# Attention on one core: scores issued three query blocks ahead instead of two

## The reference

```
q, k = rope(x @ w_aq), rope(x @ w_ak);  v = x @ w_av
s = q k^T / 128, causal mask;  p = softmax(s);  r = (p v) @ w_ao
x = layernorm(x + r)
h = silu(x W1' s1) * (x W2' s2);  h = gelu(h H1' g1);  h = gelu(h H2' g2)
x = layernorm(x + h W3' s3)
```

## Time and profile before

| what | value |
|---|---|
| three runs | 1079.12 us median (1076.83 to 1079.99) |
| the profiled execution | 1077.77 us, its span 1076.0 us |
| mean granted TensorE clock | 0.979 |
| TensorE matmul busy | 995.9 us, 93% of the span |
| VectorE busy | 852.0 us, 79% |
| ScalarE busy | 655.7 us, 61% |
| GpSimd busy | 584.5 us, 54% |
| first scores of head 0 / start of feed-forward | 29.28 us / 785.53 us |

### The profile page before, as it was taken

How to read it: one execution, slowest core, us unless ns; L and a number is a source line. 1 busy time by engine, 2 the same in 40 slices (tenths; PEclk the granted TensorE clock), 3 DMA queues, 4 the chain that set the end, 5 groups by cost and what they waited for, 6 DMA issues and landing times. The chain is left out here.

```text
span 1076.0 us, 20027 instructions
## 1 busy us (share of the span) xinstructions
PE 995.9 (93%) x5648; PEld 859.3 (80%) x5648; DVE 852.0 (79%) x1803; ACT 655.7 (61%) x1383; POOL 584.5 (54%) x536
## 2 busy tenths in 40 slices
PE   2799999999999999999999999999839999999995
PEld 1588888888888888888888888888728878788784
DVE  4888888988889898888888888888755668486744
ACT  4577676777767677777767777777625252343531
POOL 3777777777777877767787777777350101000000
PEclk8799999999999999999999999999969999999998
DMA  7542223432223223232222222221020000000000
GB/s 249 167 137 60 69 61 88 153 89 59 60 69 73 63 58 91 58 77 64 76 49 58 60 60 70 69 68 40 1 79 1 1 1 21 0 19 0 1 20 20
DMA packets 33292, 66.16 MB, mean 61 GB/s; under 512 B 5456, under 2 KB 6992, under 8 KB 32208
## 3 DMA queue, kind: packets, MB, share of 16 engines
q1 hardware_dynamic: 30400, 58.62, 20.6%
q10 hardware_dynamic: 2832, 6.82, 1.7%
HBM read 24.26 MB, written 7.34 MB: 29 GB/s over the span
## 5 line engine op out<-in xcount | busy, mean ns | idle before, releaser
L720 POOL TENSOR_SCALAR probs<-probs,inv_sum 128x128 f32<-128x128 f32 (+7 forms) x256 | 236.7, 925 | 173.5 <-DVE inv_sum L635 173.5
L537 ACT ACTIVATE pT<-psum 128x512 fp32r<-128x512 f32 (+3 forms) x384 | 176.0, 490 | 131.2 <-PE psum L404 130.1
L311 PE MATMUL psum<-pT,vals 128*128 128x512 f32 (+3 forms) x1152 | 242.2, 350 | 1.6 <-DVE rT L678 1.6
L525 ACT ACTIVATE probs<-psum,neg_max 128x128 f32<-128x128 f32 (+7 forms) x256 | 190.3, 744 | 48.8 <-DVE neg_max L629 46.9
L645 DVE TENSOR_TENSOR pT<-psum,pT 128x512 fp32r<-128x512 f32 (+3 forms) x384 | 199.8, 547 | 14.8 <-ACT pT L537 11.8
L311 PEld LDWEIGHTS psum<-pT,vals 128*128 128x128 f32 x1152 | 187.3, 189 | 24.0 <-DVE pT L645 1.7
L629 DVE TENSOR_REDUCE neg_max<-psum 128x1 f32<-128x128 f32 (+7 forms) x256 | 190.4, 744 | 3.7 <-PE psum L395 3.7
L404 PE MATMUL psum<-ident,probs 128*128 128x128 f32 x1152 | 174.6, 276 | 12.8 <-POOL probs L720 6.4
L725 POOL TENSOR_TENSOR swapped<-swapped,rope 128x512 f32<-128x512 f32 x128 | 165.4, 1292 | 37.2 <-DMA swapped<-proj 37.1
L901 PE MATMUL ps<-hid,w 128*128 128x512 f32 x768 | 181.3, 396 | 0.0
L901 PEld LDWEIGHTS ps<-hid,w 128*128 128x128 f32 x768 | 143.8, 188 | 34.4
(11 more groups left out here) (78 smaller groups left out, 1267.9 us busy)
## 6 DMA issues: line engine op xcount, KB each, us to landing
swapped<-proj SPq DMA_DIRECT2D x256, 128.0 KB, 2.3
w_stage<-qk_split SPq DMA_DIRECT2D x30, 256.0 KB, 2.6
wv_stage<-v_split SPq DMA_DIRECT2D x15, 256.0 KB, 2.6
x_split<-ffn_raw ACTq DMA_DIRECT2D x2, 1024.0 KB, 5.9
ffn_raw<-g SPq DMA_DIRECT2D x2, 1024.0 KB, 8.1
x_moving<-x_split SPq DMA_DIRECT2D x2, 1024.0 KB, 5.9
out<-y SPq DMA_DIRECT2D x4, 512.0 KB, 2.6
raw_x<-xT SPq DMA_DIRECT2D x3, 512.0 KB, 11.5
```

The costliest lines, as they stand in the source:

```text
L311: ins = nc.tensor.matmul(out_ap, left[a], right[b], start=first and i == 0, stop=last and i == 2)
L525: nc.scalar.activation(probs[:, ib % 4, :width].rearrange("p (h c) -> p h c", h=halves), score_ps[:, ib % 2, :halves, :half], ACT.Exp, bia ...
L537: nc.scalar.activation(pT[chunk][:, 0, 4 * f:4 * f + n_blocks, (ib % 4) * P:(ib % 4 + 1) * P], bank("t", head[1], nth)[:, :n_blocks * P].r ...
L720: nc.gpsimd.tensor_scalar(p, p, inv_sum[:, n:n + 1], 1.0, ALU.mult, ALU.mult).then_inc(probs_ready[0], 1)
```

## The change

LOOK = 3 takes the place of a written-out 2: TensorE issues scores of block s+3 in step s, ScalarE and VectorE follow (exp and 1/sum of block s+2, maximum of block s+3). GpSimd's product of probabilities with 1/sum stays at block s+1. Every step of the rotation moves one step forward; tile 1 and tile 2 are still projected at the steps 0 and 2, tile 0 moves to the last step of the head before, and tile 3 from step 2 to step 3. On VectorE the order inside a step is now sum of the rotation, maximum, 1/sum. The two banks are lent one step sooner, and the order in which the shared banks go round follows from the planner. One more step is put ahead of the first head.

```
+LOOK = 3
-QK_STEP = (0, 0, 2, 2)
-COS_STEP = (0, 0, 2, 2)
-SIN_STEP = (1, 2, 3, 4)
-SUM_STEP = (2, 3, 4, 6)
-HIGH_STEP = (3, 4, 6, 8)
-LOW_STEP = (3, 4, 6, 8)
+QK_STEP = (-1, 0, 2, 3)
+COS_STEP = (-1, 0, 2, 3)
+SIN_STEP = (0, 1, 3, 4)
+SUM_STEP = (1, 2, 4, 5)
+HIGH_STEP = (2, 3, 5, 6)
+LOW_STEP = (2, 3, 5, 7)
 V_STEP = (4, 5, 6, 6)
 PV0_PIECES = {6: range(0, 2), 7: range(2, 4)}
 PV1_PIECES = {1: range(0, 2), 2: range(2, 4), 3: range(4, 8)}
-LEND1 = (6, 7, 0)
-LEND3 = (1, 2)
+LEND1 = (5, 6, 7)
+LEND3 = (0, 1)
+QK_AHEAD = [1 - step // NI for step in QK_STEP]
...
-            ib, tile_off = (s + 2) % NI, off + (s + 2) // NI
+            ib, tile_off = (s + LOOK) % NI, off + (s + LOOK) // NI
...
-                     + [("qk", off + 1, j) for j in range(NQK) if QK_STEP[j] == s]
+                     + [("qk", off + QK_AHEAD[j], j) for j in range(NQK) if QK_STEP[j] % NI == s]
...
+        body((-1, 0), NI - 1, 0)
         for s in range(NI):
             body((-1, 1), s, 0)
...
 TensorE
-                if before_first(head) and s == NI - 2:
+                if before_first(head) and s == NI - LOOK:
                     pe.wait_ge(masks_ready, 1)
                     pe.wait_ge(vo_low, 1)
                 if exists(ahead):
-                    scores(ahead, (s + 2) % NI)
+                    scores(ahead, (s + LOOK) % NI)
...
 ScalarE
-                if before_first(head) and s == NI - 2:
+                if before_first(head) and s == NI - LOOK:
                     save_weights()
...
                 if exists(ahead):
-                    exponentiate(ahead, (s + 1) % NI)
+                    exponentiate(ahead, (s + LOOK - 1) % NI)
...
 VectorE
-                if exists(step_on(head, (s + 1) // NI)):
-                    inverse_sum(step_on(head, (s + 1) // NI), (s + 1) % NI)
                 for target, j in rope_tasks(head, s, SUM_STEP):
                     rope_sum(target, j)
-                if exists(step_on(head, (s + 2) // NI)):
-                    negative_max(step_on(head, (s + 2) // NI), (s + 2) % NI)
+                if exists(step_on(head, (s + LOOK) // NI)):
+                    negative_max(step_on(head, (s + LOOK) // NI), (s + LOOK) % NI)
+                if exists(step_on(head, (s + LOOK - 1) // NI)):
+                    inverse_sum(step_on(head, (s + LOOK - 1) // NI), (s + LOOK - 1) % NI)
```

More of the change, by code:

```diff
@@ L277, in before_first @@
     def before_first(head):
-        return isinstance(head[0], int) and head[0] < 0
+        return isinstance(head[0], int) and number(head) == -1
     def pair_exists(pair):
@@ L285, in bank, with qk_use @@
         return psum[:, USES[use][0] * BANK:(USES[use][0] + 1) * BANK]
+    def qk_use(head, j):
+        off = (parity(head) - QK_AHEAD[j]) % 2
+        return "qk", off + QK_AHEAD[j], j
     def wait_for_banks(pe, pair, *use):
@@ L408, in project_qk @@
             def project_qk(running, nth):
-                head = step_on(running, 1)
+                head = step_on(running, QK_AHEAD[nth])
                 if nth == 0:
@@ L454, in step @@
             def step(head, s, b):
-                ahead = step_on(head, (s + 2) // NI)
+                ahead = step_on(head, (s + LOOK) // NI)
                 if before_first(head) and s == 1:
@@ L471, in step @@
                 for target, j in rope_tasks(head, s, QK_STEP):
-                    project_qk(step_on(target, -1), j)
+                    project_qk(head, j)
                 for c in v_tasks(head, s):
@@ L546, in copy_projected @@
                 wait_for(act, rope_low, step_on(head, -1), j)
-                nc.scalar.activation(proj[:, j % 2], bank("qk", 1 if parity(head) else 2, j),
+                nc.scalar.activation(proj[:, j % 2], bank(*qk_use(head, j)),
                                      ACT.Copy).then_inc(proj_copied[0], 1)
@@ L566, in step @@
             def step(head, s, b):
-                ahead = step_on(head, (s + 1) // NI)
+                ahead = step_on(head, (s + LOOK - 1) // NI)
                 if before_first(head) and s == 1:
@@ L573, in step @@
                         high_of_x(b)
-                if before_first(head) and s == NI - 2:
+                if before_first(head) and s == NI - LOOK:
                     save_weights()
-                if before_first(head) and s == NI - 1:
+                if before_first(head) and s == NI - LOOK + 1:
                     act.wait_ge(vo_low, 1)
@@ L652, in times_cos @@
                 wait_for(dve, rope_done, step_on(head, -1), j)
-                nc.vector.tensor_tensor(by_cos[:, j], bank("qk", 1 if parity(head) else 2, j),
+                nc.vector.tensor_tensor(by_cos[:, j], bank(*qk_use(head, j)),
                                         rope[:, 0, c * BANK:(c + 1) * BANK],
```

## The result

| what | before | after |
|---|---|---|
| runs, four of each, interleaved | 1079.03 us (1076.83 to 1079.99) | 1110.32 us (1107.40 to 1114.21) |
| the profiled execution, its span | 1077.77, 1076.0 us | 1107.6, 1105.8 us |
| mean granted TensorE clock | 0.979 | 0.975 |
| first scores of head 0 | 29.28 us | 32.91 us |
| first scores of head 2 | 76.74 us | 84.96 us |

The ratio is 1.0293 with an interval of 1.0258 to 1.0328: slower by 31 us. I had forecast 1096.5 with a range of 1075 to 1114: the sign was right and the range held it, but the loss is almost twice my +17.5.

What follows compares the result with a forecast made beforehand. TensorE sets the time, and only its own waits can be won. New waits of 2.8 us a pair for 1.7 give +1.1 x 15.5 = +17, plus 0.5 for filling: 1095.3 profiled, 1096.5 on the median's scale; range 1075 to 1114.

Steps and rivals of the forecast that it cites:

- (1): Steady state: TensorE's old waits, 1.7 us a pair, go if nothing takes their place.
- (4): Even head, step 6: second fill of transposes waits for bank 1, still to be read by ScalarE; 0.5 us.
- (2): Odd head: blocks 7 and 1 share score bank 2, so block 1 waits for maximum and exp 7; 1.1 us.
- (3): Even head, step 5: second fill of transposes waits for bank 5, whose VectorE reader is late; 0.5 us.
- (5): Rotation chain through GpSimd: odd-head transposes wait 0.4 us at step 6, then 0.3; step 2 taken as nothing.
- (6): SyncE: swaps go out singly, tile 0's behind a value-projection wait and the value weights; projected early enough, so nothing.
- (7): Filling: tile 2's copy waits for the first sum, VectorE idles some 0.6 longer; +0.5 us, bounds -2 and +1.5.
- Draining: Last 24 matmuls wait for the add, through transposes 7 that come as late as before; 0, bounds -1.5 and 0.
- C: Rival: GpSimd's chain takes over, with new waits of 4.0 us a pair; +36, 1115 us; chance 0.17.
- A: Rival, faster: VectorE and ScalarE run ahead, banks come free sooner, new waits 0.9 us a pair; 1067 us; chance 0.17.
- B: Rival: only the fixed waits, (2), (3) and 0.3 of (4), 1.9 us a pair; +3, 1082 us; chance 0.20.
- D: Rival: waits make TensorE's clock fall to half for a tenth of the stretch; 1135 us; chance 0.02.

Runs made afterwards that it cites:

- sin_behind: Changed kernel with the first sin product a step later on GpSimd, behind probabilities 2 (SIN_STEP 1, 1, 3, 4): 1107.18 us, 1.0251.
- lows_first: Changed kernel with GpSimd's low part of a tile ahead of the sin product inside a step: 1099.17 us, 1.0164.
- combined: Changed kernel with lows_first's order, first sin product behind probabilities 2, odd-head p v piece in step 5, weight and x saves away from swaps: 1084.04 us, 1.004.
- dma_apart: Changed kernel with split-weight saves after head 0's last swap, x saves from step 5, feed-forward loads behind the next pair's weights: 1105.14 us, 1.024.
- look2_newrot: Changed kernel put back to scores two blocks ahead and the old bank lending, keeping the new rotation and VectorE order: 1269.39 us, 1.1746.

## Why the prediction was right in sign and short in size

**Steps (1) to (4): right.** The wait for the rotation went, and the reuse of score banks took more than it gave. (2) was 1.06 for 1.1, (3) 0.5, (4) 0.3 for 0.5. A pair was forecast at 47.3 us and takes 47.42. The terms of (2) as written give 1.99 us of work and not 1.9, so 1.0 and not 1.1; the measured 1.06 lies between.

**Step (5): right as a chain, wrong inside.** I counted the products at steps 6 and 7 at 0.7 and they cost 0.34. I took step 2 as nothing, on a difference of 8.4 against 8.3 between two sums of eight durations each, and it costs 0.7 a pair. The wait early in the head delays TensorE, so there is less left for the later ones to take: sin_behind shows this, where the 0.36 won at step 2 came back as 0.35 and 0.3 at step 5. That the new waits came out at 2.9 for 2.8 is luck as far as (5) goes: 0.36 too much at the steps 6 and 7 and 0.7 too little at step 2. With 2.0 us of old waits instead of 1.7 a pair is 0.89 longer, 12.5 us over 14 pairs (forecast 1.1 x 15.5 = 17, which counts pairs of the filling and the draining too): the miss isn't there.

**Step (6), "the DMAs: nothing": wrong.** I had moved SyncE's swaps past what stands on SyncE's own queue only. What made them late was on other queues: saves issued by ScalarE, and, on SyncE, loads of the feed-forward weights that need the DMA engines for longer than the step that was given away. Head 7 lost 2.6 us and head 1 3.6 us by it (both gone or moved when the transfers were moved). Heads 19 and 21 lost 3.8 more. In the head before head 19 the sin product of tile 2 starts 20.12 us after scores 0 (488.58), 19.18 in head 16 (440.36), since its swap was late. The sum of tile 3 then starts behind a low part on GpSimd and takes 1.71 us (494.77), where it starts ahead of it in head 16 and takes 0.68 (446.57). With GpSimd's order exchanged (lows_first) neither head is slow. The order alone doesn't settle it, though: combined has it too, and there head 19 takes 29.11 us, with the sum of tile 3 ahead of it at 1.72 us again (475.92) and 3.7 us more than usual in its steps 2 and 3.

**Step (7), "filling +0.5": wrong, +8.2.** The diff has the line `if before_first(head) and s == NI - LOOK: save_weights()`, and it is quoted ahead of the prediction. I took it as renamed and not as moved. dma_apart, which also moves the saves of x, gets 7.1 us back. My bound of +1.5 had no row of a transfer beside another in it.

**Draining, 0: too low.** The stretch from head 30 on takes 2.9 more, of which 0.9 is what any pair loses; no run was made for the other 2.0.

**The range.** That 1075 to 1114 holds the measured 1110 is in part luck. Its upper end came from C, while some 10 us of the loss (7.1 in the filling, 2.6 at head 7) are the transfers of (6) and (7), which I had put at nothing and at 0.5.

**The rivals.** C's size came about (1110 for 1115) but not by its mechanism: the steady waits were 2.9 a pair, not 4.0 (its terms with (2) and (3) add up to 4.2). A had the engines running ahead of the score banks, and 1.06 of 1.1 shows that they can't. B's fixed waits were all there, and the chain had no slack on top. For D: from 60 to 760 us, with 1 us waits in every pair, the clock row reads 1.00. The Trainium skill (TensorE: Matmul & The Clock Gate, "A second HAM failure mode: psum-queue depth-cycling") says that short idles between groups of matmuls can make the clock go to and fro; this trace doesn't agree. Where the waits were up to 3.1 us (look2_newrot) the mean was 0.96.

**Open.** What delays the swap ahead of head 19 by 0.9 us; why that head takes 29.1 us in the last version; what the last 2.0 us are; and whether the feed-forward loads fit anywhere without a cost, as two places were tried and each hit the next weights.

## What to carry to other kernels

A constant that sets how far ahead one engine runs also moves everything that is placed relative to it: look for each use of it, and for each one ask which transfers it starts and which small, urgent transfer is issued in the next 10 us. Where two chains end within a few tenths of each other, removing the one that shows gains nothing; look for where they part, as here at maximum 7, since only what ends sooner up to that point shortens both. An edit that gains nothing alone can still gain with another one (0.7 us a pair) or gain nothing again, and only the distances step by step tell which. Don't write "nothing" for a difference of 0.1 us between long sums. A wait that is removed without its chain becoming shorter usually stands a step later under another name; count the distance of a whole round, not the wait.

## What the runs showed of the hardware

**Who is held when VectorE and GpSimd start together.** A sum on VectorE (two inputs in SBUF, 0.69 us alone) often starts just behind an operation on GpSimd. In the changed kernel 33 sums started 0.07 to 0.13 us behind GpSimd's tensor_tensor, and all were held, to 1.71 to 1.77 us. Another 63 started 0.05 to 0.07 us behind its tensor_scalar: the median is 0.69 and the longest 1.18, and it is GpSimd's operation that grows. VectorE and GpSimd, in two places each:

```profile
466.57 1.77 DVE L668 TENSOR_TENSOR swapped<-by_cos,swapped 128x512 f32<-128x512 f32 x1 [0.46 <-POOL swapped L733]
...
483.32 0.69 DVE L668 TENSOR_TENSOR swapped<-by_cos,swapped 128x512 f32<-128x512 f32 x1 [0.64 <-POOL swapped L733]
```
```profile
466.50 1.29 POOL L740 TENSOR_TENSOR qk<-swapped,qk 128x512 fp32r<-128x512 f32 x1
...
483.26 1.23 POOL L728 TENSOR_SCALAR probs<-probs,inv_sum 128x512 f32<-128x512 f32 x1
```

The second product takes 1.23 where the earlier trace rows have 0.69 for an undisturbed one. The Trainium skill (SBUF — State Buffer, "🔬 SBUF: two separate sides") says that whichever of the two starts first has the shared ports for its whole instruction. The first place agrees; in the second VectorE began later and went first, and the measurement decides. How close the starts are matters here. In the traces of all 14 kernels together, 106 of 681 sums that started 0.03 to 0.07 us behind a tensor_scalar were held (over 0.9 us), and all 13 that started 0.07 to 0.25 us behind one (1.16 to 1.43 us). Behind a tensor_tensor all 22 and all 297 were held. So from 0.07 us on the traces agree with the rule for both forms; below that the start in the profile doesn't say who goes first, and the form counts.

**ScalarE's transfers leave ahead of its arithmetic.** In ScalarE's program three copies of x stand ahead of the saves of the weights. They ran from 23.49 to 26.44 us, and the first save was issued at 22.27. The last of them is:

```profile
25.39 1.05 ACT L500 ACTIVATE ffn_raw<-raw_x 128x1024 fp32r<-128x1024 f32 x1
```

The third save waits for the low part of the values' weights. VectorE ends it at 24.46 (23.24 and 1.22), and the save goes out at 24.48, ahead of a copy that is written before it. The first save had its data ready at 9.93 (VectorE's row at 9.51, 0.42 long) and went out 12 us later, so a transfer doesn't always leave when its data are ready either; what held this one is open. The step in which a transfer is written isn't its time of issue: read that from the trace.
